# attention_1 of a two-layer decoder: one pass of statistics for two norms, the residual on ScalarE, weights split two heads ahead

## The chip, the core and the metric

The kernel runs on one core of a Trainium2 chip, in one launch. The metric is the device time of that launch in microseconds (us); lower is better. The engines named below are TensorE (PE, matmuls; PEld its weight loads), VectorE (DVE), ScalarE (ACT), GpSimd (POOL) and SyncE (SP, which here only issues DMAs). Each works through its own queue in order and waits on semaphores.

## The reference

Two decoder layers on x of 4 x 256 rows of 256 numbers, six blocks in a row, each added to x. The change touches only the fourth, the attention of the second layer. Cut to it:

```python
def _layernorm(x, axis=-1, eps=1e-05):
    m = jnp.mean(x, axis=axis, keepdims=True)
    v = jnp.var(x, axis=axis, keepdims=True)
    return (x - m) / jnp.sqrt(v + eps)

def _L1_attn_ref(h, wq, bq, wk, bk, wv, bv, wo, bo, ln_g, ln_b):
    residual = h                                    # h is already _layernorm(x)
    mu = jnp.mean(h, axis=-1, keepdims=True)
    var = jnp.mean(jnp.square(h - mu), axis=-1, keepdims=True)
    x = (h - mu) * jax.lax.rsqrt(var + EPS) * ln_g + ln_b
    q, k, v = ...                                   # 16 heads of 128
    q, k = rope(q), rope(k)
    attn = causal softmax(q k / sqrt(128))
    return (attn v) @ wo.T + bo + residual

x = x + _L1_attn_ref(_layernorm(x, axis=-1), ...)
```

So there are an outer norm (of x, giving h) and an inner norm (of h), and x becomes x + h + bo + the sum over 16 heads.

## The kernel before

The 1024 rows lie as 8 tiles of 128 rows (`NT`) in `k.x`; they are handled in two halves of 4 tiles (`HALF`).

**The entry of the block.** VectorE takes the statistics of x (`row_stats`: bn_stats, then bn_aggr into `k.mv`). GpSimd turns variances into reciprocal roots (`inverse_root`, a sum with eps and a power, 128x4 numbers for a half). VectorE makes `hn` = h, takes the statistics of `hn` again, and makes `xn` in two products of three operands for each tile (L177: subtract the mean and multiply by gamma; L182: multiply by the root and add beta). TensorE turns `xn` (`turn_rows`), ScalarE rounds it into the high part `k.xs[0]`, VectorE subtracts into the low part `k.xs[1]`. All large products are three matmuls on such high and low parts (`split_product`, L142).

**Projections.** A "chunk" is one bank of 512 columns: c = 0, 1 are q, c = 2, 3 are k, c = 4 to 7 are v (of two heads at once). There are two banks `pp`, so chunk c+2 waits until chunk c has been read. For q and k, ScalarE writes the halves exchanged (`swap`, two activations, L1723), VectorE multiplies by the cosine and sine tables (`rope`, L1793 on the bank and L1795 on two tiles in SBUF), and GpSimd adds the two (`project`, L1670, the semaphore `chunk`). For head 0 this stands ahead of the loop, and there VectorE also forms x + bo + hn after each rope (`base_tile`, L1783 and L1785, two tiles after each of four chunks).

**The heads.** `step(H)` is one head; the steps 1 to 14 are a hardware loop of seven rounds of two (`heads`), steps 0 and 15 stand outside. Each step has four blocks b, one for each batch entry. In block b TensorE does the scores of (H, b), turns the probabilities of the block before (`turn_P`, L1925), does one or two chunks of head H+1 (`CHUNKS`: q in b = 0, k in b = 1, one chunk of v each in b = 2 and 3), projects out the block two before (`project_out`, three-matmul products on `OT`), and weighs v with the block before (`weigh`). ScalarE copies the turned probabilities, does the exponentials of (H, b) (L1747, L1749), the swaps, and the high part of `OT`. VectorE does the row maxima (L1803, L1805), the low part of `OT` (L135), the ropes, v's bias, and the sum into x (`add_y`, L1834).

**Weights.** SyncE fetches, for each head, `w` (q and k weights and biases, 257 KB) and `wo` (128 KB), and `wv` (256 KB) for each two heads, into one or two buffers. ScalarE rounds each to a high part (`w_to_high`, `wo_to_high`), GpSimd subtracts to the low part (`low`, L1661). In step H the casts of the weights of H+1 are the first thing on ScalarE, and their low parts the first on GpSimd; TensorE's first chunk of the step waits for the low part (`w_split`). On SyncE the order of each round is wv, w (even), wo (even), w (odd), wo (odd); a `wo` waits for `added` of the head before last, so it and everything queued behind it goes out after block 1 of a step.

## Time and profile before

| what | value |
| --- | --- |
| time, three runs | 1245.62, 1249.98, 1250.1 us; median 1249.98 |
| profiled execution | 1249.12 us, its span 1247.3 us |
| TensorE matmul busy | 1052.3 us, 84% of the span |
| VectorE / ScalarE / GpSimd busy | 802.0 / 646.6 / 448.6 us |
| granted TensorE clock, mean | 0.939 of full speed |
| attention_1 in the span | from 662.7 us (first statistics) to 1014.9 us (last sum into x) |

Times in the rows are us from the start of the span; a duration of a merged row covers all its instructions (x4 is four). "idle before" in square brackets is how long the engine had nothing to do just before, and who released it. The attention's tiles show as sb_a_..., since the program's names are shown without numbers.

### The profile page before, as it was taken

To read this page: it belongs to the slowest core of one execution; us is meant where nothing else is said; L and a number is where in the kernel's file an instruction comes from. 1 tells how busy PE (TensorE), PEld (TensorE's weight loads), DVE (VectorE), ACT (ScalarE), POOL (GpSimd) and SP (SyncE) were. 2 spreads that over 40 slices of the span, in tenths; PEclk is the share of its full clock that TensorE was granted. 3 is DMA by queue.
4 is the path that set the end of the run, shared out by engine and by line. 5 is a ranking of instruction groups with operands and counts; after the bars stand their busy time and mean duration, and the time that the engine had idled before them with its cause. 6 is when DMAs were issued, how large, how long until landed. Compare 5 with 4: busy or idle time off the path is not lost. (4 is left out here: it accounts for less than half of the span.)

```text
span 1247.3 us, 21375 instructions
## 1 busy us (share of the span) xinstructions
PE 1052.3 (84%) x7014; PEld 833.8 (67%) x7016; DVE 802.0 (64%) x2260; ACT 646.6 (52%) x1583; POOL 448.6 (36%) x408
## 2 busy tenths in 40 slices
PE   4789999999988986699993799999999977786767
PEld 3556666666665655588882588788887855575556
DVE  5656666666644565355557867677676745489983
ACT  2166676766663751243331566767676642234532
POOL 5456565655634331000002433433343300106730
PEclk8999999999998996799996899999999998898878
DMA  4250212101005000444430001010110000000001
GB/s 135 66 162 18 52 44 51 44 19 35 2 2 193 1 2 0 91 117 111 105 71 13 9 14 34 21 34 17 30 34 21 17 1 0 1 26 26 26 28 45
DMA packets 27246, 53.54 MB, mean 43 GB/s; under 512 B 4565, under 2 KB 11797, under 8 KB 26788
## 3 DMA queue, kind: packets, MB, share of 16 engines
q1 hardware_dynamic: 27172, 52.60, 15.5%
q8 instruction: 41, 0.67, 0.2%
q14 instruction: 33, 0.27, 0.1%
HBM read 42.56 MB, written 1.63 MB: 35 GB/s over the span
## 5 line engine op out<-in xcount | busy, mean ns | idle before, releaser
L382 POOL TENSOR_TENSOR sb_a_P<-sb_a_P,sb_a_rec 128x512 f32<-128x512 f32 x128 | 130.5, 1040 | 134.7 <-DVE sb_a_rec L572 134.7
L459 ACT ACTIVATE sb_a_P<-sb_a_nS,sb_a_nm 128x257 f32<-128x257 f32 x256 | 129.0, 509 | 24.4 <-DVE sb_a_nm L561 24.3
L561 DVE CUSTOM_DVE_ANT_0 sb_a_nS<-a_pS,sb_a_mask,sb_a_nsink 128x256 f32<-128x256 f32 x256 | 107.7, 479 | 15.5 <-PE a_pS L685 15.5
L1723 ACT ACTIVATE sb_a_t<-a_pp,sb_a_w 64x512 f32<-64x512 f32 x128 | 87.5, 684 | 49.4 <-PE a_pp L142 48.1
L468 ACT COPY sb_xn<-a_pT 128x512 f32<-128x512 f32 x128 | 73.7, 576 | 74.7 <-PE a_pT L699 74.5
L142 PE MATMUL a_pp<-sb_x_high,sb_a_w_low 128*128 128x512 f32 x188 | 87.1, 464 | 29.2 <-POOL sb_a_w_low L1661 20.3
L699 PE MATMUL a_pT<-sb_ident,sb_a_P 128*128 128x128 f32 x512 | 82.0, 283 | 18.4 <-ACT sb_xn L468 10.5
L1793 DVE SCALAR_TENSOR_TENSOR sb_a_t<-a_pp,sb_a_w,sb_a_cs 128x512 f32<-128x512 f32 x64 | 47.8, 746 | 73.9 <-ACT sb_a_t L1723 73.9
L699 PEld LDWEIGHTS a_pT<-sb_ident,sb_a_P 128*128 128x128 f32 x512 | 54.4, 142 | 52.1 <-issue 42.0
L142 PE MATMUL a_pY<-sb_a_wo_high,sb_a_OT_low 128*128 128x256 f32 x256 | 79.2, 309 | 7.6 <-DVE sb_a_OT_low L135 5.3
L130 ACT CAST sb_a_OT_high<-a_pO 128x256 fp32r<-128x256 f32 (+1 forms) x96 | 42.6, 444 | 78.1 <-PE a_pO L1936 39.2
L142 PE MATMUL a_pp<-sb_x_low,sb_a_w_high 128*128 128x512 f32 x188 | 76.1, 405 | 0.0
L142 PE MATMUL a_pp<-sb_x_high,sb_a_w_high 128*128 128x512 f32 x188 | 75.8, 403 | 0.0
L1670 POOL TENSOR_TENSOR sb_a_qT<-sb_a_t 128x512 f32<-128x512 f32 x32 | 41.3, 1291 | 91.8 <-DVE sb_a_t L1795 91.8
L142 PE MATMUL a_pY<-sb_a_wo_low,sb_a_OT_high 128*128 128x256 f32 x256 | 71.7, 280 | 0.0
L142 PE MATMUL a_pY<-sb_a_wo_high,sb_a_OT_high 128*128 128x256 f32 x256 | 71.5, 279 | 0.0
L142 PEld LDWEIGHTS a_pp<-sb_x_high,sb_a_w_low 128*128 128x128 f32 x188 | 36.6, 195 | 48.7 <-issue 24.8
L709 PE MATMUL a_pO<-sb_xn,sb_a_v 128*64 128x256 f32 x512 | 68.8, 392 | 0.0
L685 PE MATMUL a_pS<-sb_a_kr,sb_a_qT 32*128 32x256 f32 x1024 | 64.3, 387 | 1.1 <-DMA sb_a_kr<-sb_a_kall 1.1
L195 POOL MEMSET sb_minus_half<- 128x8 f32 x6 | 0.6, 104 | 179.0 <-POOLq L116 178.7
L516 DVE SCALAR_TENSOR_TENSOR sb_xT<-a_pp,sb_a_w,sb_a_cos 128x512 f32<-128x512 f32 x30 | 22.5, 751 | 64.1 <-PE a_pp L142 64.1
L685 PEld LDWEIGHTS a_pS<-sb_a_kr,sb_a_qT 32*128 32x128 f32 x1024 | 49.3, 184 | 15.6 <-issue 11.9
(359 smaller groups left out, 3242.8 us busy)
## 6 DMA issues: line engine op xcount, KB each, us to landing
sb_m_cw<-m_table SPq DMA_DIRECT2D x17, 512.0 KB
sb_a_kr<-sb_a_kall SPq DMA_DIRECT2D x56, 128.0 KB, 2.4
sb_f_w<-f_w SPq DMA_DIRECT2D x12, 384.0 KB, 3.0
sb_m_gu<-m_gu SPq DMA_DIRECT2D x17, 256.0 KB, 6.5
sb_a_w<-a_w SPq DMA_DIRECT2D x16, 257.0 KB, 2.7
sb_m_dn<-m_dn SPq DMA_DIRECT2D x17, 128.0 KB, 6.7
sb_a_w<-a_w SPq DMA_DIRECT2D x8, 259.0 KB, 2.7
sb_a_wo<-a_wo SPq DMA_DIRECT2D x8, 256.0 KB, 2.6
```

Of the source, the lines that this page charges most:

```text
L130: return nc.scalar.copy(out, x)
L142: ins = nc.tensor.matmul(out, a[p], b[q], start=start and i == 0, stop=stop and i == 2, **kw)
L382: nc.gpsimd.tensor_tensor(part, part, rec[b % 2][:, h, :].rearrange("p (q o) -> p q o", o=1) .to_broadcast([P, 2, S]), ALU.mult).then_inc( ...
L459: out = nc.scalar.activation(Pm[b % 2][:, h, qt, 0:S + 1], nS[:, h, qt, 0:S + 1], ACT.Exp, bias=nm[b % 2][:, h, qt:qt + 1], scale=-1.0, ac ...
L468: nc.scalar.copy(PT[h], pT[:, :]).then_inc(PT_ready, 1)
L561: out = nc.vector.tensor_tensor_reduce(nS[:, h, qt, 0:S], pS[h][:, qt * S:(qt + 1) * S], wmask[:, qt, :], -1.0, nsink[par][:, h:h + 1], AL ...
L685: out = nc.tensor.matmul(pS[h][:, qt * S:(qt + 1) * S], qT[par][e][strip, c:c + P], kr[par][e][strip, b * S:(b + 1) * S], start=(e == 0), ...
L699: out = nc.tensor.transpose(pT[:, (2 * c + qt) * P:(2 * c + qt + 1) * P], Pm[b % 2][:, h, qt, c * P:(c + 1) * P], k.tile["ident"][:, :])
L709: out = nc.tensor.matmul(pO[h * A0_D:(h + 1) * A0_D, p * S:(p + 1) * S], values_at(G, 2 * b + c), PT[2 * p + h][:, c * S:(c + 1) * S], sta ...
L1670: nc.gpsimd.tensor_tensor(dst[:, half * NC:(half + 1) * NC], t1[c % 2][:, :, :].rearrange("p b s -> p (b s)"), t2[c % 2][:, :, :].rearrang ...
L1723: out = nc.scalar.activation(t2[n][a, :, :].rearrange("p b s -> p (b s)"), pp[n][b, :], ACT.Identity, bias=bias[b])
L1793: nc.vector.scalar_tensor_tensor(out=t1[n][:, :, :], in0=pp[n][:, :].rearrange("p (b s) -> p b s", b=2), scalar=bias, in1=table(0), op0=AL ...
```

## The change

- The inner norm's statistics are no longer taken from `hn`. From the mean m and variance V of x alone, h = (x - m) r with r = (V + eps)^-1/2, and the inner norm is (x - m) times (V (1 + eps) + eps^2)^-1/2. GpSimd makes both roots in one power on 128x2x4 numbers for each half (`spread2`, `root2`), and VectorE makes `xn` from x in two products a tile. The tile `hn`, its scaling and its statistics are gone.
- x + h is formed as x (1 + r) - m r by one ScalarE activation a tile (`grow`), with `grown` and `shift` made by VectorE; bo is added by GpSimd, eight sums after head 0's last `project` (L1712). VectorE's `base_tile` is gone. VectorE still waits for all eight (`based`) ahead of the first step.
- Weights are split earlier. ScalarE casts `w` of head H+2 in block 2 of step H, `wo` of head H+1 in block 3, and `wv` in block 1 of odd steps. GpSimd makes the low parts of `w` and `wo` after the four projects of H+1, and that of `wv` between the second and the third. The first two heads' `w`, `wv` and `wo` of head 0 are split at the entry. SyncE's order and waits are unchanged.
- The loop now holds steps 1 to 12; the steps 13, 14 and 15 are written out.

```diff
@@ heads
-            with eng.Fori(0, (A1_H - 2) // 2) as i:
+            with eng.Fori(0, (A1_H - 4) // 2) as i:
...
-            step(A1_H - 1, 1, last=True)
+            for H in range(A1_H - 3, A1_H):
+                step(H, H % 2, last=(H == A1_H - 1))
@@ gpsimd
-            for turn in range(2):
-                inverse_root(nc, pool, k, ln, rstd_ready, turn)
+            exponents = k.minus_half[:, :].rearrange("p (a n) -> p a n", a=2)
+            for half in range(2):
+                cols = slice(half * HALF, (half + 1) * HALF)
+                pool.wait_ge(ln, (half + 1) * 2 * HALF)
+                nc.gpsimd.tensor_scalar(spread2[:, 0, cols], k.mv[:, cols, 1], LN_EPS, None, ALU.add)
+                nc.gpsimd.tensor_scalar(spread2[:, 1, cols], k.mv[:, cols, 1], 1.0 + LN_EPS, LN_EPS * LN_EPS,
+                                        ALU.mult, ALU.add).then_inc(rstd_ready, 1)
+                pool.wait_ge(rstd_ready, root_ready(0, half) - 1)
+                nc.gpsimd.tensor_tensor(root2[:, :, cols], spread2[:, :, cols], exponents, ALU.pow).then_inc(rstd_ready, 1)
...
-                if not last:
-                    w_low(H + 1, 1 - par)
-                    if par == 1:
-                        low(wv_high, H + 3, wv[:, :], wvs, wv_split, 2)
-                low(wo_high, H + 1, wo[par][:, 0:D], wos[par], wo_split)
-                if not last:
-                    project(H + 1, 1 - par)
+                project(H + 1, 1 - par, (0, 1))
+                if par == 1:
+                    low(wv_high, H + 3, wv[:, :], wvs, wv_split, 2)
+                project(H + 1, 1 - par, (2, 3))
+                if more(H, 2):
+                    w_low(H + 2, par)
+                wo_low(H + 1, 1 - par)
@@ scalar, entry
+            w_to_high(1, 1)
+            wo_to_high(0, 0)
+                act.wait_ge(shifts, half + 1)
+                for t in range(half * HALF, (half + 1) * HALF):
+                    nc.scalar.activation(k.x[:, t, :], k.x[:, t, :], ACT.Identity, bias=shift[:, t:t + 1],
+                                         scale=grown[:, t:t + 1]).then_inc(grown_x, 1)
@@ vector
-                row_scale(nc, dve, k, k.x, hn, rstd_ready, 0, half, h_ready)
-                dve.wait_ge(h_ready, (half + 1) * HALF)
-                row_stats(nc, dve, k, hn, ln, 1, half)
...
-                nc.vector.tensor_tensor(k.x[:, t, :], k.x[:, t, :], rows[:, 2, :], ALU.add).then_inc(based, 1)
-                dve.wait_ge(based, NT + 2 * t + 1)
-                nc.vector.tensor_tensor(k.x[:, t, :], k.x[:, t, :], hn[:, t, :], ALU.add).then_inc(based, 1)
```

How this moves instructions, at three places. First GpSimd at the entry, ahead of head 0's projections; before:

```order
L202 TENSOR_SCALAR sb_ve<-sb_mv 128x4
L204 TENSOR_TENSOR sb_rstd<-sb_ve,sb_minus_half 128x4
L1661 TENSOR_TENSOR sb_a1_w0_low<-sb_a1_w0,sb_a1_w0_high 128x512
L1661 TENSOR_TENSOR sb_a1_wv_low<-sb_a1_wv0,sb_a1_wv_high 128x512
L1670 TENSOR_TENSOR sb_a1_qT0<-sb_a1_t10,sb_a1_t20 128x512
```

and now:

```order
L1673 TENSOR_TENSOR sb_a1_root2<-sb_a1_spread2,sb_minus_half 128x2x4
L1677 TENSOR_TENSOR sb_a1_w0_low<-sb_a1_w0,sb_a1_w0_high 128x512
L1677 TENSOR_TENSOR sb_a1_wv_low<-sb_a1_wv0,sb_a1_wv_high 128x512
L1677 TENSOR_TENSOR sb_a1_w1_low<-sb_a1_w1,sb_a1_w1_high 128x512
L1677 TENSOR_TENSOR sb_a1_wo0_low<-sb_a1_wo0,sb_a1_wo0_high 128x256
L1689 TENSOR_TENSOR sb_a1_qT0<-sb_a1_t10,sb_a1_t20 128x512
```

Four low parts instead of two now stand between the last power and the first projection's sum.

Second, ScalarE in the loop, from block 3 of one step into block 0 of the next (Pm is the exponential's output, OT the weighed values, PT the turned probabilities); before:

```order
L1749 ACTIVATE sb_a1_Pm1,sb_a1_den3<-sb_a1_nS1,sb_a1_nm1 128x256
L130 CAST sb_a1_OT0_high<-a1_pO0 128x256
L130 CAST sb_a1_w1_high<-sb_a1_w1 128x512
L130 CAST sb_a1_wo0_high<-sb_a1_wo0 128x256
L1741 COPY sb_a1_PT1<-a1_pT 128x384
```

and now the same cast of w stands in block 2 of the step before, ahead of the high part of OT:

```order
L1776 ACTIVATE sb_a1_Pm0,sb_a1_den2<-sb_a1_nS0,sb_a1_nm0 128x256
L1624 ISA
L1723 REGISTER_ALU
L130 CAST sb_a1_w1_high<-sb_a1_w1 128x512
L130 CAST sb_a1_OT1_high<-a1_pO1 128x256
L1768 COPY sb_a1_PT0<-a1_pT 128x384
```

The cast has moved back by some two blocks, and OT's high part stands directly behind it (the two rows without a tile compute what the cast waits for).

Third, GpSimd in an odd step of the loop, now:

```order
L1689 TENSOR_TENSOR sb_a1_qT0<-sb_a1_t11,sb_a1_t21 128x512
L1676 REGISTER_ALU
L1677 TENSOR_TENSOR sb_a1_wv_low<-sb_a1_wv0,sb_a1_wv_high 128x512
L1687 REGISTER_ALU
L1689 TENSOR_TENSOR sb_a1_kT0<-sb_a1_t10,sb_a1_t20 128x512
```

where before wv's low part stood ahead of all four projections:

```order
L1661 TENSOR_TENSOR sb_a1_w0_low<-sb_a1_w0,sb_a1_w0_high 128x512
L1660 REGISTER_ALU
L1661 TENSOR_TENSOR sb_a1_wv_low<-sb_a1_wv0,sb_a1_wv_high 128x512
L1660 REGISTER_ALU
L1661 TENSOR_TENSOR sb_a1_wo1_low<-sb_a1_wo1,sb_a1_wo1_high 128x256
```

It now falls between q's second sum and k's first.

## Rows read from the trace of the kernel before

**Rows 1.** Waits of TensorE from 704 to 1000 us: total, times, longest

```profile
PE a_pp L142 <- POOL sb_a_w_low L1661: 20.3, 14, 1.5
```

**Rows 2.** Timeline, TensorE: turned probabilities and the chunk behind; start, us

```profile
865.34 0.49 PE L1925 MATMUL a_pT<-sb_ident,sb_a_Pm 128*128 128x128 f32 x3
865.59 0.48 PE L142 MATMUL a_pp<-sb_x_high,sb_a_w_low 128*128 128x512 f32 x1
...
878.13 0.49 PE L1925 MATMUL a_pT<-sb_ident,sb_a_Pm 128*128 128x128 f32 x3
880.10 0.50 PE L142 MATMUL a_pp<-sb_x_high,sb_a_w_low 128*128 128x512 f32 x1 [1.47 <-POOL sb_a_w_low L1661]
```

**Rows 3.** Timeline, ScalarE's cast and GpSimd's low part ahead of that chunk

```profile
878.08 0.62 ACT L130 CAST sb_a_w_high<-sb_a_w 128x512 fp32r<-128x512 f32 x1
...
878.77 1.27 POOL L1661 TENSOR_TENSOR sb_a_w_low<-sb_a_w,sb_a_w_high 128x512 fp32r<-128x512 f32 x1 [3.97 <-ACT sb_a_w_high L130]
```

**Rows 4.** Timeline, SyncE: w issued, odd and even step; its landing (L1647)

```profile
852.47 0.33 SPq L1647 DMA_DIRECT2D sb_a_w<-a_w  x1
...
873.21 0.33 SPq L1647 DMA_DIRECT2D sb_a_w<-a_w  x1
...
DMA to landing us min/median/max: 2.6/2.7/3.0
```

**Rows 5.** Timeline, ScalarE in block 2 of those two steps

```profile
853.15 0.19 ACT L1749 ACTIVATION_READ_ACCUMULATOR sb_a_Pm<-sb_a_nS,sb_a_nm 128x1 f32 x1
...
872.68 0.19 ACT L1749 ACTIVATION_READ_ACCUMULATOR sb_a_Pm<-sb_a_nS,sb_a_nm 128x1 f32 x1
873.89 0.37 ACT L130 CAST sb_a_OT_high<-a_pO 128x256 fp32r<-128x256 f32 x1 [1.03 <-PE a_pO L1936]
```

**Rows 6.** Timeline, block 3: VectorE's low part of OT and TensorE's use

```profile
875.35 0.42 DVE L135 TENSOR_TENSOR sb_a_OT_low<-a_pO,sb_a_OT_high 128x256 fp32r<-128x256 f32 x1
...
876.11 0.28 PE L142 MATMUL a_pY<-sb_a_wo_high,sb_a_OT_low 128*128 128x256 f32 x1
```

**Rows 7.** Timeline: the third rope's second half, and v's chunk behind it

```profile
869.76 0.68 DVE L1795 TENSOR_TENSOR sb_a_t<-sb_a_t,sb_a_cs 128x512 f32<-128x512 f32 x1
...
870.71 0.37 PE L142 MATMUL a_pp<-sb_a_wv_high,sb_x_low 128*128 128x256 f32 x1
```

**Rows 8.** Timeline, VectorE at the entry: four products of each kind

```profile
672.44 1.64 DVE L177 SCALAR_TENSOR_TENSOR sb_xn<-sb_a_hn,sb_mv,sb_a_rows 128x256 f32<-128x256 f32 x4
674.00 3.69 DVE L182 SCALAR_TENSOR_TENSOR sb_xn<-sb_xn,sb_rstd,sb_a_rows 128x256 f32<-128x256 f32 x4
```

**Rows 9.** Timeline, GpSimd beside them

```profile
673.06 1.11 POOL L204 TENSOR_TENSOR sb_rstd<-sb_ve,sb_minus_half 128x4 f32<-128x4 f32 x1
674.15 1.45 POOL L1661 TENSOR_TENSOR sb_a_w_low<-sb_a_w,sb_a_w_high 128x512 fp32r<-128x512 f32 x1
675.56 1.44 POOL L1661 TENSOR_TENSOR sb_a_wv_low<-sb_a_wv,sb_a_wv_high 128x512 fp32r<-128x512 f32 x1
```

**Rows 10.** Groups of GpSimd, whole span: busy us, mean ns, idle before

```profile
L412 POOL TENSOR_TENSOR sb_x<-sb_x,sb_a_bo 128x256 f32<-128x256 f32 x8 | 5.6, 733 | 0.0
```

**Rows 11.** Groups from 600 to 1000 us: the swaps and the ropes

```profile
L1723 ACT ACTIVATE sb_a_t<-a_pp,sb_a_w 64x512 f32<-64x512 f32 x128 | 87.5, 684 | 49.4 <-PE a_pp L142 48.1
...
L1793 DVE SCALAR_TENSOR_TENSOR sb_a_t<-a_pp,sb_a_w,sb_a_cs 128x512 f32<-128x512 f32 x64 | 47.8, 746 | 73.9 <-ACT sb_a_t L1723 73.9
L1795 DVE TENSOR_TENSOR sb_a_t<-sb_a_t,sb_a_cs 128x512 f32<-128x512 f32 x64 | 43.6, 681 | 0.0
```

**Rows 12.** Timeline: TensorE's first chunk, VectorE's first row maxima

```profile
682.10 0.80 PE L142 MATMUL a_pp<-sb_x_high,sb_a_w_low 128*128 128x512 f32 x1 [0.42 <-DVE sb_x_low L135]
...
704.27 0.28 DVE L1803 CUSTOM_DVE_ANT_0 sb_a_nS<-a_pS,sb_a_mask 128x128 f32<-128x128 f32 x1
```

**Rows 13.** Timeline, VectorE: a base tile beside GpSimd's sum, and the statistics' end

```profile
665.90 0.38 DVE L156 BATCH_NORM_AGGREGATE sb_mv<-sb_stats 128x2 f32<-128x6 f32 x4
...
688.03 1.40 DVE L1785 TENSOR_TENSOR sb_x<-sb_x,sb_a_hn 128x256 f32<-128x256 f32 x1
```

More of the change, by code:

```diff
@@ L1603, in exists, with more @@
             return not ((first and b < lag) or (drain and b >= lag))
+        def more(H, n):
+            return not isinstance(H, int) or H + n < A1_H
         def before(H, c, n):
@@ L1664, in w_low, with wo_low, project @@
                 low(w_high, X + 1, w[par][:, 0:2 * KD * P], ws[par], w_split)
-            def project(X, par):
-                for c in range(4):
+            def wo_low(X, par):
+                low(wo_high, X + 1, wo[par][:, 0:D], wos[par], wo_split)
+            def project(X, par, cc=range(4)):
+                for c in cc:
                     pool.wait_ge(roped, X * 4 + (c + 1))
@@ L1675, in step @@
             def step(H, par, first=False, last=False, drain=False):
-                if drain:
+                if drain or last:
                     return
-                if not last:
-                    w_low(H + 1, 1 - par)
-                    if par == 1:
-                        low(wv_high, H + 3, wv[:, :], wvs, wv_split, 2)
-                low(wo_high, H + 1, wo[par][:, 0:D], wos[par], wo_split)
-                if not last:
-                    project(H + 1, 1 - par)
+                project(H + 1, 1 - par, (0, 1))
[5 more added lines that the diff above has]
+                wo_low(H + 1, 1 - par)
             w_low(0, 0)
             low(wv_high, 2, wv[:, :], wvs, wv_split, 2)
+            w_low(1, 1)
+            wo_low(0, 0)
             project(0, 0)
+            for t in range(NT):
+                pool.wait_ge(grown_x, t + 1)
+                nc.gpsimd.tensor_tensor(k.x[:, t, :], k.x[:, t, :], rows[:, 2, :], ALU.add).then_inc(based, 1)
             heads(pool, step)
@@ L1709, in _, with grow @@
             high_of(nc, wvs[0][:, :], wv[:, :]).then_inc(wv_high, 2)
-            for j in (0, 2, 1, 3):
-                act.wait_ge(turned, (j % NH2) + 1)
-                high_of(nc, part_of(k.xs[0], j), turn_banks[j][:, :]).then_inc(x_high, 1)
+            w_to_high(1, 1)
+            wo_to_high(0, 0)
+            def grow(half):
+                act.wait_ge(shifts, half + 1)
+                for t in range(half * HALF, (half + 1) * HALF):
+                    nc.scalar.activation(k.x[:, t, :], k.x[:, t, :], ACT.Identity, bias=shift[:, t:t + 1],
+                                         scale=grown[:, t:t + 1]).then_inc(grown_x, 1)
+            for half in range(2):
+                grow(half)
+                act.wait_ge(turned, half + 1)
+                for j in (half, 2 + half):
+                    high_of(nc, part_of(k.xs[0], j), turn_banks[j][:, :]).then_inc(x_high, 1)
             def swap(X, par, c):
@@ L1751, in step @@
                             .then_inc(probs, 1)
+                    if not drain and not last:
+                        if b == 1 and par == 1:
+                            act.wait_ge(wv_in, H * 8 + 8)
+                            act.wait_ge(proj, H * 6 + 6)
+                            high_of(nc, wvs[0][:, :], wv[:, :]).then_inc(wv_high, 2)
+                        if b == 2 and more(H, 2):
+                            w_to_high(H + 2, par)
+                        if b == 3:
+                            wo_to_high(H + 1, 1 - par)
                     if len(cc) > 0 and cc[0] < 4:
```

40 lines of the change are left out of this document (22 added, 18 removed).

## The prediction

> **What bounds the kernel now.** I read the list of waits first, TensorE's alone, over the heads of this attention. One line holds nearly all of it: 14 waits, 20.3 us together, for the low part of the next head's weights [rows 1]. TensorE has no other idle row there, so in this stage TensorE sets the pace and this wait lies on its path. The timeline gives its true price. Without a wait a chunk starts 0.25 us behind the turned probabilities (865.34 to 865.59), with it 1.97 us behind (878.13 to 880.10), so one costs 1.72 us [rows 2]. Its cause is on the page: a cast of 0.62 and a subtraction of 1.27, both begun only at the turn of the step [rows 3]. The second bound is the entry: VectorE is busy almost without a break from 662.8 on, TensorE's first chunk starts at 682.10, and the first row maxima stand at 704.27 [rows 12].
>
> **The change part by part.**
>
> *The wait on the split weights* goes in steps 1 to 14: 14 x 1.72 = 24.1 us [rows 1, 2]. The low parts now start behind the last project of a step, blocks ahead of their use.
>
> *What is late next: the transfer.* SyncE's order is unchanged, so w of head H+2 is still issued only after the sum of block 1 in step H, and now ScalarE wants it in block 2 of the same step. In an even step it is issued at 873.21 and lands 2.7 us later, at 875.9 [rows 4]; ScalarE's exponentials end at 872.87 [rows 5]. Both hang on the same sum of VectorE, so this distance of 3.0 us does not shrink when TensorE gets faster. Behind the waiting cast stands OT's high part. It moves from 873.89 to 875.9 + 0.52 (the cast, until the next can start) = 876.45. Its 0.37 and the low part's 0.42 with two handovers put TensorE's use at 877.3, where it now starts at 876.11 [rows 5, 6]: 1.2 us late. Chunk 5 or 7 of TensorE covers the rest. In an odd step wv is not in between: issue at 852.47, landing 855.2, exponentials over at 853.34 [rows 4, 5], a wait of 1.8; OT's low part is then there at 856.6. TensorE would ask at 856.5 (876.11 less one head; the exponentials lie 19.5 apart [rows 5]), so it is some 0.15 late. Steps 2 to 12, even: 6 x 1.2 = 7.2. Steps 1 to 13, odd: 7 x 0.15 = 1.1. Step 0 has its w long before, step 14 has none to cast. By the row's ends (2.6 and 3.0 us of landing) this sum is 7.4 and 12.
>
> *wv in block 1 of odd steps.* Its cast of some 0.52 stands ahead of the third swap, and its low part of 1.27 to 1.29 on GpSimd lies beside the third rope's second product, which reads two tiles from SBUF. Such a product beside a GpSimd subtraction takes 1.40 instead of 0.42 (one base tile [rows 13]). Here the two overlap only at the end; I reckon 0.15. So the third rope ends 0.67 late. The slack is small: it ends at 870.44 and v's chunk starts at 870.71 [rows 7], so 0.4 reaches TensorE, and VectorE's queue carries the rest to the low part of OT behind it. Bounds: nothing (if the cast falls into idle time) and 0.52 + 0.98; taken 0.65, since slack is shown to be only 0.27. 7 x 0.65 = 4.6.
>
> Loop: 24.1 - 7.2 - 1.1 - 4.6 = 11.2 us gained.
>
> *The entry up to the first chunk.* Statistics end at 666.2 [rows 13]. VectorE then has 16 products at 1.64 for four, 6.5 us in all, and small ones of 0.4, where it now has these plus the scaling and second statistics. Alone they would end at 672.9. But four GpSimd subtractions (some 1.3, 1.3, 1.3 and 0.7 us) now run beside them, from the end of the second power at about 668.4. Rows: beside two of those subtractions four products took 3.69 instead of 1.64 [rows 8, 9], 1.0 for each. Four cost 4.0 at that rate; bounds 2.0 (if only two meet products) and 4.6 (their whole length). The power on 8 numbers a row is not in the trace; 1.11 is that of 4 [rows 9], so it is between 1.1 and 2.2; VectorE works on the first products meanwhile, so it decides only when the subtractions begin. The first two low parts of x follow, 1.2 us: first chunk at 672.9 + 4.0 + 1.2 = 678.1 instead of 682.1 [rows 12]. Gain 4.0.
>
> A rule speaks of the same resource. By the row, GpSimd's power of 1.11 at 673.06 did not stretch the four products of 1.64 beside it, while its subtractions did [rows 8, 9]. The Trainium skill, "SBUF — State Buffer", section "Who interferes with whom", has VectorE with two SBUF inputs and any GpSimd instruction that reads SBUF exclude each other for the whole instruction. Were that so for the powers too, products would stand still for one or both of them and this gain would be 1 to 2.5 us smaller; the row decides against it.
>
> *From the first chunk to the first maxima:* 22.2 us now [rows 12]. The base tiles leave VectorE, up to 1.40 + 0.42 each [rows 13]. What is left is a ring: chunk about 1.5 (2.7 for the first, whose matmul shows 0.80 against 0.50 us [rows 2, 12]), swap 2 x 0.68, rope 0.75 + 0.68 [rows 11], then TensorE's next chunk into the same bank. Up to the first rope's end 2.8 + 1.4 + 1.4 = 5.6; one turn of the ring (4.4) later the third, at 10.0; the fourth 2.0 behind; GpSimd's last sum 1.3 more: 13.3. But now eight sums of bo stand behind it, 8 x 0.733 = 5.9 [rows 10], and VectorE waits for all of them before its first maxima: 19.2. Gain 3.0. In step 0 ScalarE no longer trails base tiles, which I count as 0.5. If VectorE did not have to wait, 5 more would be gained; the wait is in the program, so they are not.
>
> *ScalarE's eight activations on x* (some 0.4 each) lie in its idle time before the turned tiles arrive, and the two extra casts at the entry too: nothing, or at most 0.5 if the second half's four hold up the rounding. The small VectorE operations are in the 0.4. Steps 13 and 14 written out instead of looped: nothing, no stall shows in step 15 now.
>
> **Sum:** 11.2 + 4.0 + 3.5 = 18.7 us. The profiled execution took 1249.1 us (span 1247.3), so it would take 1230.4; the median of the runs lies 0.9 above it, which gives 1231.
>
> **The rivals.**
>
> *The weights come in time, or GpSimd hinders less.* If the cast did not wait, 8.3 fewer are lost; if wv's parts are hidden, 4.6; if the subtractions at the entry cost half, 2. With the first and half of the rest it is about 1249.98 - 18.7 - 11.5 = 1220. For it: TensorE's slack in these blocks is only estimated. Against: issue and exponentials hang on one VectorE sum, 0.3 us apart, against 2.7 of landing.
>
> *The casts' wait passes whole to TensorE.* ScalarE's lateness, less the 1.03 it idles there today [rows 5], is 2.5 in even steps and 1.3 in odd ones: 6 x 2.5 + 7 x 1.3 = 24.1, as much as was removed. Less the 4.6 it leaves 2.9 to 7.5 us of the entry: 1242 to 1247, middle 1245. It needs the exponentials of block 3, behind the same cast, to be what TensorE waits for; they are used a block later, which speaks against it.
>
> *Slower: the transfer misses its turn and feeds itself.* The landing rows hold for bursts that ScalarE does not wait on. If ScalarE's lateness delays VectorE's sums, these delay SyncE's `wo`, w goes out later, and the cast waits again. Each us past the slack costs TensorE nearly one in 13 steps. Zero gain is reached at a landing of 2.7 + 18.7 / 13 = 4.1 us; at 4.8 it is 1258. The rows end at 3.0 [rows 4], and the sum of block 1 does not stand behind the cast of block 2, so the ring is broken within a step.
>
> *It does not do what it says:* the wait stays because w's low part is late for another reason. By the rows it is ready at 875.9 + 0.65 + 1.27 = 877.8 in an even step, and the first chunk of the next would stand at 878.4 + 1.2 = 879.6 [rows 2 to 4]: 1.7 us in hand, so a landing of 4.4 us would bring it back.
>
> **How the numbers follow.** The forecast (1226 to 1238) 0.62; in time or less hindrance, 1220, 0.18; whole wait passed on, 1245, 0.12; slower, 1258, 0.05; the wait stays, about 1243 to 1250, 0.03. The range takes the first two and the faster edge of the third: 1219 to 1243. About 0.5% is what a measurement here can tell from no change, so under 1243.7 is faster: 0.62 + 0.18 + 0.04 of the third = 0.84. Within 0.5%: 0.08 + 0.03 = 0.11. Slower: 0.05.
>
> **What would show it.** Right: no wait of the first chunk for the low weights; in block 2 ScalarE's cast of w with 3.0 us idle in even steps and 1.8 in odd, released by the DMA; TensorE idle about 1.2 us before the second projection out of even steps, and 0.3 to 0.4 before v's first chunk of odd ones; first chunk at 678; eight sums of 0.73 on GpSimd with VectorE idle before its first maxima; a head 0.8 us shorter on average (11.2 / 14). Wrong: a cast without idle time, products at the entry near 0.4 us each, or a landing above 3.0 us. Then the time goes to 1220, or to 1245 and above.

## The result, and the profile after the change

The changed kernel takes 1232.47 us (median of four runs, 1230.88 to 1235.94) against 1250.04 us for the kernel before: a ratio of 0.9871, 95% interval 0.9841 to 0.9902. The forecast was 1231 us with a range of 1219 to 1243. The total came out as forecast, but the sum behind it did not: the loop gave 6.4 us instead of 11.2. Why the total was met all the same comes first, since it decides how everything else is read.

**The total holds a part that the change did not make.** The change touches nothing ahead of this attention's norms. Yet these norms, whose first instruction is VectorE's first statistics (line 153), began at 662.76 us in the profile of before and at 659.08 in that of after. A second trace of each kernel (both under the experiments) began at 664.01 and 663.85, and over all 14 profiles of this study the start lies between 658.87 and 664.01, in no order by kernel. So I measure the stage by itself: from its first statistics to the first statistics of the stage behind it. Here are the two rows for before, then for after. Timelines give start, length, engine, line, operation, and in brackets the idle time before and what ended it.

```profile
662.76 1.40 DVE L153 BATCH_NORM_STATS2 sb_stats<-sb_x 128x6 f32<-128x256 f32 x4 [1.99 <-PEq L116]
...
1015.46 1.41 DVE L153 BATCH_NORM_STATS2 sb_stats<-sb_x 128x6 f32<-128x256 f32 x4 [0.53 <-PEq L1536]
```

```profile
659.08 1.41 DVE L153 BATCH_NORM_STATS2 sb_stats<-sb_x 128x6 f32<-128x256 f32 x4 [1.99 <-PEq L116]
...
999.00 1.41 DVE L153 BATCH_NORM_STATS2 sb_stats<-sb_x 128x6 f32<-128x256 f32 x4 [0.53 <-PEq L1536]
```

The stage took 352.70 us and takes 339.92: **12.8 us gained, where the sum said 18.7.** The other 3.7 us between the two profiles were there before the changed code ran. The stages behind it take 231.8 us in both (span less the second row).

Inside the stage I mark each step by its first row maxima (their start in block 0 of head H; [rows 12] have the first of them). "Step H" below is the time from head H's mark to head H+1's. All in us, from the timelines:

| | first chunk after start | first maxima after start | step 0 | steps 1, 3 .. 13 (sum of 7) | steps 2, 4 .. 12 (sum of 6) | step 14 | stage |
|---|---|---|---|---|---|---|---|
| before | 19.34 | 41.51 | 17.45 | 137.47 | 117.53 | 19.56 | 352.70 |
| after | 14.94 | 34.22 | 18.35 | 133.54 | 116.56 | 18.04 | 339.92 |
| gained | 4.40 | 7.29 | -0.90 | 3.93 | 0.97 | 1.52 | 12.78 |

Three views of after say where the rest of the 24 us went. First the waits of TensorE and of ScalarE between 704 and 990 us (total, times, longest), to be held against [rows 1]:

```profile
PE a_pY L142 <- DVE sb_a_OT_low L135: 10.2, 10, 1.5
PE a_pp L142 <- DVE sb_a_t L1833: 3.0, 7, 0.5
...
ACT sb_a_w_high L130 <- DMA sb_a_w<-a_w: 32.9, 13, 3.5
```

The wait for w's low part is gone, all 14 of it. Two others stand in its place on TensorE (of the 10.2 us, 7.2 are six waits in even steps and 0.16 one in step 1; the other three, 0.94 each, belong to the last head, which shows them in the kernel before as well), and ScalarE now waits 32.9 us for the transfer of w. Then the timeline, the parts that answer to [rows 4] to [rows 7]: an even step from w's issue to the projection out, and an odd one.

```profile
859.38 0.33 SPq L1656 DMA_DIRECT2D sb_a_w<-a_w  x1
862.17 0.62 ACT L130 CAST sb_a_w_high<-sb_a_w 128x512 fp32r<-128x512 f32 x1 [3.13 <-DMA sb_a_w<-a_w]
862.69 0.37 ACT L130 CAST sb_a_OT_high<-a_pO 128x256 fp32r<-128x256 f32 x1
863.57 0.39 PE L142 MATMUL a_pY<-sb_a_wo_high,sb_a_OT_low 128*128 128x256 f32 x1 [1.12 <-DVE sb_a_OT_low L135]
...
875.80 1.03 DVE L1833 TENSOR_TENSOR sb_a_t<-sb_a_t,sb_a_cs 128x512 f32<-128x512 f32 x1
876.96 0.38 PE L142 MATMUL a_pp<-sb_a_wv_high,sb_x_low 128*128 128x256 f32 x1 [0.47 <-DVE sb_a_t L1833]
881.40 0.62 ACT L130 CAST sb_a_w_high<-sb_a_w 128x512 fp32r<-128x512 f32 x1 [2.07 <-DMA sb_a_w<-a_w]
```

Even step: ScalarE idles 3.13 us in front of the cast of w, OT's high part stands behind that cast, and TensorE waits 1.12. Odd step: the rope's second product takes 1.03 us, where it took 0.68 [rows 7], and v's chunk starts 0.47 late; ScalarE's wait for w is 2.07.

Last the entry, which answers to [rows 8, 9, 12]: VectorE's products, GpSimd beside them, and what follows.

```profile
665.81 4.70 DVE L1819 SCALAR_TENSOR_TENSOR sb_xn<-sb_xn,sb_a_root,sb_a_rows 128x256 f32<-128x256 f32 x4
670.43 0.69 DVE L1815 TENSOR_SCALAR sb_a_grown<-sb_a_root 128x4 f32<-128x4 f32 x1
674.02 0.80 PE L142 MATMUL a_pp<-sb_x_high,sb_a_w_low 128*128 128x512 f32 x1 [0.42 <-DVE sb_x_low L135]
...
693.30 0.29 DVE L1841 CUSTOM_DVE_ANT_0 sb_a_nS<-a_pS,sb_a_mask 128x128 f32<-128x128 f32 x1 [4.63 <-POOL sb_x L1712]
695.01 0.90 PE L1961 MATMUL a_pT<-sb_ident,sb_a_Pm 128*128 128x128 f32 x3 [2.96 <-ACT sb_a_Pm L1776]
697.80 0.80 PE L142 MATMUL a_pp<-sb_x_high,sb_a_w_low 128*128 128x512 f32 x1 [1.89 <-DVE sb_a_t L1833]
```

VectorE idles 4.63 us for GpSimd's eight sums before its first maxima. TensorE then waits 2.96 and 1.89, and its matmul of 128x512 takes 0.80 us (0.50 at [rows 2]). Step 0 became longer by these waits and by the granted clock behind them: it was half (the lower level, 1.2 GHz) in the two us from 697 on, columns as in the windows view (length, busy of PE, PEld, DVE, ACT, POOL, then the clock, the DMA's share and GB/s):

```profile
697.00:699.00 2.00, 1.20 (x3) 1.01 (x4) 2.00 (x8) 1.90 (x6) 1.17 (x1) 0.50 0.00 0
```

### The profile page after: what moved, and what is told of

The parts are those of the page before. It is cut to its first block and busy times, and to the rows that moved or that the text cites. A ratio compares the mean times of both kernels' runs of the same rounds, so it can differ in the third digit from the quotient of the medians.

```text
span 1230.8 us, 21280 instructions
## 1 busy us (share of the span) xinstructions
PE 1050.8 (85%) x7014; PEld 829.6 (67%) x7016; DVE 791.5 (64%) x2224; ACT 649.0 (53%) x1591; POOL 453.7 (37%) x414
## 5 line engine op out<-in xcount | busy, mean ns | idle before, releaser
L142 PEld LDWEIGHTS a_pY<-sb_a_wo_high,sb_a_OT_low 128*128 128x128 f32 x256 | 48.2, 188 | 25.0 <-DVE sb_a_OT_low L135 22.7
L135 DVE TENSOR_TENSOR sb_a_OT_low<-a_pO,sb_a_OT_high 128x256 fp32r<-128x256 f32 (+1 forms) x96 | 49.0, 511 | 23.7 <-ACT sb_a_OT_high L130 20.1
```

The source lines that it names most:

```text
L135: return nc.vector.tensor_tensor(out, x, high, ALU.subtract)
L142: ins = nc.tensor.matmul(out, a[p], b[q], start=start and i == 0, stop=stop and i == 2, **kw)
```

## The experiments

Twelve kernels were run: ten variants, and the kernel before and the changed one once more. Each is read by the stage's length and its steps, which do not contain what differs from run to run ahead of the stage; the ratio to the kernel before stands beside it (none where a kernel was timed in one execution only). From the first statistics, in us:

| kernel | first chunk | first maxima | step 0 | odd (7) | even (6) | step 14 | stage | ratio, 95% |
|---|---|---|---|---|---|---|---|---|
| before, second trace | 19.35 | 41.69 | 17.27 | 137.29 | 117.47 | 19.51 | 352.37 | |
| changed, second trace | 14.94 | 34.24 | 18.38 | 133.93 | 116.30 | 18.05 | 340.13 | 0.9885 (0.9867 to 0.9903) |
| w first | 14.94 | 34.20 | 18.42 | 131.63 | 107.72 | 18.04 | 329.25 | 0.9828 (0.9804 to 0.9851) |
| wv at the top | 14.93 | 34.21 | 18.48 | 127.91 | 116.01 | 18.03 | 333.88 | 0.9841 (0.9806 to 0.9875) |
| wait put off | 14.93 | 29.68 | 17.20 | 133.89 | 116.14 | 18.04 | 334.18 | 0.9855 (0.9827 to 0.9884) |
| these three | 14.93 | 29.32 | 17.24 | 125.70 | 107.71 | 18.04 | 317.25 | 0.9707 (0.9682 to 0.9733) |
| w first, cast of wv at the top | 14.94 | 34.20 | 18.38 | 131.55 | 107.73 | 18.05 | 329.14 | |
| w later | 14.93 | 34.23 | 18.49 | 149.31 | 137.66 | 18.05 | 376.97 | 1.0221 (1.0194 to 1.0249) |
| low parts later at the entry | 13.40 | 34.15 | 18.53 | 134.00 | 116.20 | 18.03 | 340.15 | |
| norms only | 13.40 | 32.19 | 20.02 | 138.27 | 117.69 | 19.56 | 346.94 | 0.9925 (0.9900 to 0.9949) |
| weights only | 20.83 | 42.47 | 16.73 | 133.93 | 116.32 | 17.86 | 346.47 | 0.9928 (0.9902 to 0.9955) |
| all four edits | 13.40 | 27.67 | 19.08 | 125.72 | 107.75 | 18.05 | 317.52 | 0.9717 (0.9692 to 0.9741) |

**How far the stage's length can be trusted.** Both kernels once more.

> The kernel before, once more, for a second trace of it. Theory (the 3.7 us by which the attention stage began earlier in the changed kernel's profile come from executions that differ, since no instruction ahead of it was changed): its first statistics start anywhere from 659 to 663.5 us, and the stage takes 352.7 us within 0.3. Rival (the stage itself scatters that much): a stage length more than 1 us away from 352.7.

> The changed kernel, once more, for a second trace and more rounds on this chip. Theory: first statistics anywhere from 659 to 663.5 us, the stage 339.9 us within 0.7 (its odd and even steps hang on transfers that scatter by some 0.1 us each), a ratio of 0.985 to 0.990 to the kernel before. Rival (the stage scatters as the total does): a stage more than 1.5 us away from 339.9.

The stage repeats within 0.33 us (352.70 and 352.37, a hair outside the 0.3 I had named) and 0.21 us (339.92 and 340.13). The starts were 664.01 and 663.85, 0.4 to 0.5 us outside the range that I had given, and the ratio is 0.9885. So the change is worth 12.2 to 12.8 us, about 1.0%, which lies inside both intervals of the ratio (12.5 / 1249 is a ratio of 0.990). The 3.7 us belong to those two executions and not to the change. Earlier marks, the first statistics of the stages ahead, say where they arise: at 378.34 and 377.65 the two profiles were 0.7 us apart, at 478.97 and 475.34 already 3.6. The windows view of the same ten us of that stage, before and then after, shows what differs, TensorE's granted clock:

```profile
398.34:408.34 10.00, 10.00 (x58) 6.51 (x58) 4.64 (x10) 6.57 (x9) 3.31 (x3) 0.69 0.00 0
```

```profile
397.65:407.65 10.00, 10.00 (x92) 6.73 (x93) 6.81 (x16) 8.25 (x12) 4.13 (x3) 1.00 0.00 0
```

A clock of 0.69 for ten us takes 3.1 us of work away, about the 2.9 by which the stage is longer. Over the 14 profiles three have the low clock at this place (before, changed second trace, wait put off) and take 100.6 to 100.8 us there; the other eleven have 1.00 and take 97.7 to 98.9. Why the clock falls there in some executions of equal code stays open.

**Is it the transfer?** w leaves a head earlier. SyncE's transfers stand in three functions here, with the waits that they had; w of head 2 is issued ahead of the loop, and the last round is written out.

```diff
+            fetch_w(2, 0)
             with sp.Fori(0, (A1_H - 4) // 2) as i:
                 fetch_wv(i)
                 for s in range(2):
-                    fetch_w(i * 2 + (2 + s), s)
+                    fetch_w(i * 2 + (3 + s), 1 - s)
                     fetch_wo(i * 2 + (2 + s), s)
```

> The changed kernel, but SyncE issues w of head H+3 before it waits with wo of head H+2, so w leaves a whole head earlier; nothing else is moved and nothing is left out. Theory (the late transfer is what the loop lost): ScalarE's 32.9 us of idle time before its 13 casts of w go to nearly nothing; the 6 even steps, which lost 1.39 us each against a step without a new wait, get it back (8.3 us), and the odd ones a small part (0 to 2 us): the attention stage takes 330 to 332 us instead of 339.9, the whole kernel 8 to 10 us less than the changed one, a ratio of about 0.979 to the kernel before. Rival (the casts themselves hurt where they stand now, ahead of the exponentials of block 3, and the wait for the DMA only covers that): the idle time goes too, but the stage gets less than 3 us shorter, 337 us or more.

The six even steps fell from 116.56 to 107.72 (8.8 us, 17.95 each), the seven odd ones from 133.54 to 131.63 (1.9). The stage is 10.7 us shorter, a little more than the 8 to 10 expected, and ScalarE has no wait for a DMA left between 704 and 985 us. TensorE's waits, in the list from 720 to 960 us, are down to the odd steps' one:

```profile
PE a_pp L142 <- DVE sb_a_t L1849: 3.0, 7, 0.5
```

The theory holds: the late transfer cost 8.8 us in even steps and 1.9 in odd ones. The casts themselves, where they stand, cost nothing once their data is there.

**And if w comes later still?** 128 KB into a spare buffer, waited for, ahead of each w.

```diff
+                    sp.dma_start(spare[:, :], src["a1_wo"][0]).then_inc(spare_in, 16)
+                    sp.wait_ge(spare_in, (h - 1) * 16)
                     sp.dma_start(w[s][:, :], src["a1_w"][bass.ds(h, 1)].rearrange("g p n -> p (g n)"))\
```

> The changed kernel, but ahead of every w SyncE first brings 128 KB into a spare buffer and waits until they are there, which took 2.0 us for wo in the trace of the changed kernel: w lands about 2.1 us later in each of the 13 steps that fetch one. Nothing is left out. Theory (no slack is left, and the delay is paid once per step, one for one, as the prediction's slower rival has it from a landing of 4.1 us on): 13 x 2.1 = 27 us on the stage, 365 to 369 us instead of 339.9, the kernel slower than the one before, about 1258 us. The cast of w then waits some 2 us longer, and in even steps the first chunk's wait for w's low part comes back. Rival (the wait feeds itself: each late w makes the next one later still): more than 35 us, with waits for the DMA that grow from step to step. Rival (ScalarE's lateness is mostly covered): less than 14 us.

The kernel is slower than the one before, 1274.63 us, ratio 1.0221; the stage takes 376.97 us, 37.1 more than the changed one. Expected were 27, so this missed, and by size it fits the rival that feeds itself. By its own sign it does not: the even steps take 23.38, 23.10, 23.01, 22.81, 22.85 and 22.51 us and the odd ones 21.05 to 21.67, with no growth. The rows tell the two parts apart: issue, cast, use of OT in an even step, and the first matmul behind it.

```profile
880.87 0.33 SPq L1659 DMA_DIRECT2D sb_a_w<-a_w  x1
883.51 0.62 ACT L130 CAST sb_a_w_high<-sb_a_w 128x512 fp32r<-128x512 f32 x1 [5.38 <-DMA sb_a_w<-a_w]
884.91 0.39 PE L142 MATMUL a_pY<-sb_a_wo_high,sb_a_OT_low 128*128 128x256 f32 x1 [3.38 <-DVE sb_a_OT_low L135]
885.72 0.97 PE L1973 MATMUL a_pO<-sb_a_PT,sb_a_v 128*128 128x256 f32 x2
...
886.00:888.00 2.00, 2.00 (x8) 1.76 (x7) 0.80 (x2) 0.37 (x1) 0.73 (x1) 0.50 0.00 0
```

ScalarE's wait rose from 3.13 to 5.38 in this even step; over all of them it rose by 2.25 on average in the even steps (32.7 us in six against 19.2) and by 2.06 in the odd ones (28.1 in seven against 13.6). One for one that makes 6 x 2.25 + 7 x 2.06 = 27.9 us, about the amount expected. The odd steps paid 2.25 each (15.8 / 7), 0.2 above their delay, the even ones 3.52 (21.1 / 6), 1.3 above theirs. The larger excess has TensorE's clock in it: behind the idle time of 3.38 us the clock granted is 0.50 from 886 to 888 and 0.70 from 888 to 890, which takes 1.0 + 0.6 = 1.6 us of work away. The wait of the odd step ahead of it is 2.00 us (at 863.30), and its clock stays at 1.00:

```profile
863.30:865.30 2.00, 2.00 (x14) 1.92 (x15) 1.49 (x4) 1.37 (x6) 1.30 (x2) 1.00 0.00 0
```

All thirteen are alike: behind the six waits of the even steps (3.37 to 3.62 us) the clock fell to 0.50, behind the seven of the odd steps (1.95 to 2.22 us) it never left 1.00. So the slower rival of the prediction had the price of a us nearly right (2.25 paid for 2.06 where the clock held), but not the feeding back on itself that it was named for, and it lacked the second price behind a long wait. Its last worry, w's low part late again, did not come true: TensorE has no wait for it here.

**What do wv's two parts cost?** Both back at the top of odd steps.

```diff
+                if not drain and not last and par == 1:
+                    act.wait_ge(wv_in, H * 8 + 8)
+                    act.wait_ge(proj, H * 6 + 6)
+                    high_of(nc, wvs[0][:, :], wv[:, :]).then_inc(wv_high, 2)
...
-                project(H + 1, 1 - par, (0, 1))
                 if par == 1:
                     low(wv_high, H + 3, wv[:, :], wvs, wv_split, 2)
+                project(H + 1, 1 - par, (0, 1))
```

> The changed kernel, but in odd steps the cast of wv and its low part stand at the top of the step again, where the kernel before has them, ahead of all projects; nothing is left out. Theory (wv in block 1 costs 0.65 us an odd step, as the prediction has it, and more by the steps after: 1.04 us each in all): the stage gets 4 to 5 us shorter (335 to 336 us), all of it in the 7 odd steps. Rival (the odd steps lose their 1.04 us to w's cast, which waits 2.0 us for its transfer there too): less than 1.5 us.

The odd steps fell by 5.6 us (133.54 to 127.91, 0.80 each), the stage by 6.0. That is more than the 4 to 5 expected and far from the rival's 1.5. With w first the same thing reads more clearly: odd steps 131.63, against 125.70 with both edits, are 0.85 each. To see which of the two parts it is, w first with only ScalarE's cast at the top:

```diff
+                if not drain and not last and par == 1:
+                    act.wait_ge(wv_in, H * 8 + 8)
+                    act.wait_ge(proj, H * 6 + 6)
+                    high_of(nc, wvs[0][:, :], wv[:, :]).then_inc(wv_high, 2)
```

> The changed kernel with w issued a head earlier, and of wv's two parts only ScalarE's cast back at the top of odd steps; GpSimd's low part stays between the second and the third projection. Nothing is left out. Odd steps took 18.82 us with both parts in block 1 and 17.96 with neither. Theory (ScalarE's cast, 0.61 us ahead of the third swap, is the larger part, as the prediction has it with 0.52 against 0.15): odd steps 18.1 to 18.3 us. Rival (GpSimd's low part, which holds up the rope's second product by 0.35 and the third projection behind it, is the larger part): 18.4 us or more.

The odd steps did not move: 131.55 against 131.63. My theory fell and the rival holds: with the low part where it is, moving the cast gives nothing back, and the 0.85 us go only when the low part moves too. (The cast alone in block 1, with the low part out of the way, was not run, so what it would cost by itself stays open.) The rows show how. GpSimd's subtraction and VectorE's second product of the third rope, first with the cast in block 1 (w first), then with the cast at the top:

```profile
868.57 1.03 DVE L1849 TENSOR_TENSOR sb_a_t<-sb_a_t,sb_a_cs 128x512 f32<-128x512 f32 x1
...
867.76 1.29 POOL L1693 TENSOR_TENSOR sb_a_wv_low<-sb_a_wv,sb_a_wv_high 128x512 fp32r<-128x512 f32 x1
```

```profile
871.04 1.54 DVE L1849 TENSOR_TENSOR sb_a_t<-sb_a_t,sb_a_cs 128x512 f32<-128x512 f32 x1
...
870.75 1.28 POOL L1693 TENSOR_TENSOR sb_a_wv_low<-sb_a_wv,sb_a_wv_high 128x512 fp32r<-128x512 f32 x1
```

The subtraction ends at 869.05 and at 872.03, the product at 869.60 and at 872.58, so in both 0.55 us behind the subtraction. Without the cast in its way the product starts half a us sooner within the step and is held half a us longer. A product with two inputs in SBUF makes next to no headway while GpSimd subtracts, and does most of its 0.68 afterwards. It is so in all seven odd steps of both kernels: the product ends 0.54 to 0.56 us behind the subtraction. The Trainium skill, "SBUF — State Buffer", section "Who interferes with whom", says the same: of a VectorE instruction with two SBUF inputs and a GpSimd instruction that reads SBUF, the one issued second waits until the other is through. In these traces, where GpSimd's subtraction is the one issued first, it holds.

**What does the early wait for bo's sums cost?**

```diff
+                if isinstance(H, int) and H == 0:
+                    dve.wait_ge(based, NT)
                 if not before(H, u, A1_U):
                     dve.wait_ge(added, H * A1_U + u)
...
-            dve.wait_ge(based, NT)
             heads(dve, step)
```

> The changed kernel, but VectorE's wait for the eight sums of bo stands directly ahead of its first addition to x (head 0, block 0) instead of ahead of its first row maxima; nothing is left out. Theory (the wait itself holds up step 0, since VectorE idles 4.63 us there): the first maxima come 3.5 to 4.5 us earlier, TensorE's idle time behind them in step 0 (2.96 and 1.89 us) and its half clock go with it, and the stage gets 3.5 to 5 us shorter. Rival (the wait only moves: VectorE then waits in block 0 of head 0, because GpSimd does these sums ahead of the next head's projections, which TensorE and ScalarE need anyway): less than 1.5 us shorter.

The first maxima come 4.5 us sooner (29.68 instead of 34.22 behind the start), and step 0 takes 17.20 instead of 18.35. The stage is 5.7 us shorter, above the 3.5 to 5 expected. Nothing waits for these sums later, and the matmul that took 0.80 us takes 0.50 at full clock:

```profile
692.22 0.29 DVE L1841 CUSTOM_DVE_ANT_0 sb_a_nS<-a_pS,sb_a_mask 128x128 f32<-128x128 f32 x1
...
697.14 0.50 PE L142 MATMUL a_pp<-sb_x_high,sb_a_w_low 128*128 128x512 f32 x1 [1.33 <-DVE sb_a_t L1833]
```

The prediction had the 5 us in hand ("the wait is in the program, so they are not" gained) but not that the same wait also lengthens step 0. How the 1.15 us of step 0 divide between the waits and the clock is not shown.

**Do GpSimd's subtractions hold up the entry?** Two of the four go behind the projections of head 0.

```diff
-            w_low(1, 1)
-            wo_low(0, 0)
             project(0, 0)
+            w_low(1, 1)
+            wo_low(0, 0)
```

> The changed kernel, but GpSimd makes the low parts of w of head 1 and of wo of head 0 behind the projections of head 0 instead of ahead of them; nothing is left out. Theory (each GpSimd subtraction beside VectorE's products at the entry holds them up by about 1 us; there were four, now two meet them): the four products that took 4.70 us take 3.6 to 3.9, the small scaling behind them 0.16 instead of 0.69, and TensorE's first chunk starts 13.2 to 13.6 us behind the first statistics instead of 14.94. The first row maxima do not move by more than 1 us, since they wait for the eight sums of bo, which now stand 2.3 us of other work later in GpSimd's queue: the stage stays within 1 us of 339.9. Rival (the products are long for another reason, such as ScalarE's activations on the same x): they stay at 4.7 us and the first chunk at 14.9.

```profile
666.52 3.69 DVE L1819 SCALAR_TENSOR_TENSOR sb_xn<-sb_xn,sb_a_root,sb_a_rows 128x256 f32<-128x256 f32 x4
670.13 0.15 DVE L1815 TENSOR_SCALAR sb_a_grown<-sb_a_root 128x4 f32<-128x4 f32 x1
673.19 0.79 PE L142 MATMUL a_pp<-sb_x_high,sb_a_w_low 128*128 128x512 f32 x1 [0.42 <-DVE sb_x_low L135]
...
693.94 0.29 DVE L1841 CUSTOM_DVE_ANT_0 sb_a_nS<-a_pS,sb_a_mask 128x128 f32<-128x128 f32 x1 [6.52 <-POOL sb_x L1712]
```

All as the theory said: 3.69 us instead of 4.70, 0.15 instead of 0.69, the first chunk 13.40 behind the start, and nothing won, since VectorE now idles 6.52 for the sums (stage 340.15).

**The two halves of the change.**

> Only the norms' part of the change: one pass of statistics, x formed by ScalarE and GpSimd; the weights are split as in the kernel before, at the top of a step. Nothing is left out. Theory (the two parts are separate, and the entry is worth what its rows say): from the first statistics to the first maxima 33 to 34.5 us instead of 41.5, steps 1 to 14 as before (19.6 each, 274.6), the stage 343 to 347 us instead of 352.7. Rival (the gain at the entry rests on the split two heads ahead, since otherwise w's low part stands behind eight sums of bo in step 0): step 0 takes 20 us or more instead of 17.45, and the stage 348 us or more.

> Only the weights' part of the change, on the kernel before: heads' weights split two steps ahead in blocks 1 to 3, norms and residual as in the kernel before. Nothing is left out. Theory (the loop is worth 6.4 us by the rows: 14 waits of 1.65 gone, late transfers and wv take 16 back): steps 1 to 14 together 268 us, as in the changed kernel; the entry up to 1.5 us longer, by two more GpSimd subtractions beside VectorE; the stage 345.5 to 348 us. Rival (the losses in the loop belong to the changed entry, for instance a shifted beat between VectorE and SyncE): steps 1 to 14 near 17.96 each, 252 us, and the stage under 333 us.

Norms alone gain 5.8 us (352.70 to 346.94), weights alone 6.2 (to 346.47); together 12.0, and the change gains 12.8. Steps 1 to 14 of norms alone take 275.5 us, 1.0 more than before, which nothing here explains. Weights alone have the loop of the changed kernel (133.93 + 116.32 + 17.86 = 268.1 in steps 1 to 14, as the theory had it), so its losses do not come from the new entry. At the entry it loses 1.5 us up to the first chunk, the same four products taking 4.70 us there too. Norms alone reach the first maxima at 32.19, earlier than the 33 to 34.5 expected, but half of the rival is true: step 0 takes 20.02, because w's low part for head 1 stands behind the eight sums and TensorE waits for it.

```profile
696.71 0.77 PE L142 MATMUL a_pp<-sb_x_high,sb_a_w_low 128*128 128x512 f32 x1 [5.78 <-POOL sb_a_w_low L1676]
...
689.84 5.50 POOL L1709 TENSOR_TENSOR sb_x<-sb_x,sb_a_rows 128x256 f32<-128x256 f32 x8
```

So the split of head 1 at the entry costs the norms 1.5 us up to the first chunk and 2.0 up to the first maxima (34.22 against 32.19), and spares them 1.7 in step 0 (18.35 against 20.02). Up to head 1's first maxima that is 52.57 against 52.21: at this place it is no gain.

**The three edits together.** w first, wv's parts at the top, the wait put off.

> The changed kernel with all three edits: w issued a head earlier, wv's parts back at the top of odd steps, VectorE's wait for bo's sums put off to its first addition; nothing is left out. Theory (three separate losses that add): the sum of the three, 15 to 19 us off the stage (321 to 325 us instead of 339.9), 1213 to 1217 us for the kernel, ratio 0.972 to 0.975 to the kernel before. Rival (they share one cover, and with one of them gone VectorE or ScalarE sets the pace of a head): at most 11 us, and every step 1 to 13 ends at one length of about 18.5 us or more.

The stage takes 317.25 us, 22.7 less than the changed kernel; the three alone gave 10.7 + 6.0 + 5.7 = 22.4. They add in full, which is more than I had dared to expect, and the kernel takes 1211.86 us, ratio 0.9707 (0.9682 to 0.9733). Three marks of it, and the windows view of the loop (busy of PE first):

```profile
816.34 0.29 DVE L1857 CUSTOM_DVE_ANT_0 sb_a_nS<-a_pS,sb_a_mask 128x128 f32<-128x128 f32 x1 [0.64 <-PE a_pS L1970]
834.31 0.29 DVE L1857 CUSTOM_DVE_ANT_0 sb_a_nS<-a_pS,sb_a_mask 128x128 f32<-128x128 f32 x1 [0.66 <-PE a_pS L1970]
852.27 0.29 DVE L1857 CUSTOM_DVE_ANT_0 sb_a_nS<-a_pS,sb_a_mask 128x128 f32<-128x128 f32 x1 [0.66 <-PE a_pS L1970]
...
720.00:960.00 240.00, 240.00 (x1558) 215.62 (x1556) 181.40 (x562) 181.50 (x460) 102.37 (x86) 1.00 0.10 28
```

Steps 1 to 13 take 17.91 to 17.97 us each and TensorE is busy for all of the 240 us. This is the loop with TensorE never idle, the measure for what each wait really cost.

**And the fourth edit on top** (the two low parts behind the projections of head 0):

> All three edits (w issued a head earlier, wv's parts at the top of odd steps, VectorE's wait put off) and the fourth, the two low parts behind the projections of head 0; nothing is left out. Theory (with VectorE's early wait gone, an earlier first chunk reaches the first maxima): first maxima about 1.5 us earlier than without the fourth, stage 315.5 to 316.5 us against 317.25, kernel 1209 to 1212 us. Rival (the low parts for head 1, now later, make step 0 longer by as much): no difference, 317 us or more.

The first maxima come 1.65 us earlier (27.67 against 29.32) and step 0 takes 1.84 longer: 317.52 us, no gain. The rival holds. Its step 0 shows where: the chunk of head 1 waits for w's low part, later ones for the ropes.

```profile
691.09 0.47 PE L142 MATMUL a_pp<-sb_x_high,sb_a_w_low 128*128 128x512 f32 x1 [0.37 <-POOL sb_a_w_low L1693]
695.70 0.49 PE L142 MATMUL a_pp<-sb_x_high,sb_a_w_low 128*128 128x512 f32 x1 [0.59 <-DVE sb_a_t L1849]
702.22 0.39 PE L142 MATMUL a_pp<-sb_a_wv_high,sb_x_low 128*128 128x256 f32 x1 [1.82 <-DVE sb_a_t L1849]
```

## Why the prediction was right, and where its steps were not

| term of the sum | predicted | measured | from |
|---|---|---|---|
| 14 waits for w's low part | 24.1 | 23.11 | steps 1 to 14, before (274.56) less the three edits (251.45) |
| transfer of w, even steps | -7.2 | -8.84 | after less w first |
| transfer of w, odd steps | -1.1 | -1.91 | after less w first |
| wv in block 1 | -4.6 | -5.94 | w first (257.39) less the three edits (251.45) |
| entry to first chunk | 4.0 | 4.40 | after |
| first chunk to first maxima | 3.0 | 2.89 | after |
| step 0 | 0.5 | -0.90 | after |
| sum | 18.7 | 12.81 | stage |

**The waits** went as said. Their price was a little high: 1.65 us each, by steps of 19.6 against 17.96, where two gaps in the trace had given 1.72. ("TensorE has no other idle row there" is too strong: the same view of 704 to 1000 us has two more rows, 2.2 and 0.9 us, one wait each. Both lie outside steps 1 to 14, and the sum does not use them.)

**The transfer** was the right mechanism, and its signs in the trace were as forecast: ScalarE idle 3.13 us in even steps (3.0 forecast) and 2.07 in odd ones (1.8), TensorE 1.12 us late before the projection out (1.2). What failed is the last step of the working, that TensorE's lateness at OT is the price. The waits shown were 1.03 to 1.47 us in the even steps, 7.2 together, just what the sum has (6 x 1.2), but an even step cost 1.47 on average (8.8 / 6). In odd steps "some 0.15 late" was really 0.27 (1.9 / 7), and only the first of the seven shows a wait for it, 0.16. (A slip beside it: at a landing of 2.6 us the working gives 7.0, not 7.4.) The row of a wait gives less than the wait costs. In this loop it is so for each kind: 1.45 shown and 1.65 paid for w's low part, 0.43 shown and 0.85 paid for v's chunk (3.0 / 7). What makes up the rest was not traced.

**wv** was sized at 0.65 an odd step and cost 0.85, and the working behind it was wrong in both halves. The cast, taken at 0.52 on the path, cost nothing measurable beside the low part; GpSimd's low part, taken at 0.15 because "the two overlap only at the end", was the one that held the product. I had let the product and the subtraction share, a factor on the overlap. In fact one stands still for the other, and the end of the product hangs on the end of the subtraction. (The row that the working rests on, 1.40 us in [rows 13], stands beside one of GpSimd's sums, not a subtraction; the effect is the same.)

**The entry** was right in its mechanism and nearly in size: four products 3.06 us late and a small scaling 0.53 late, together 3.6 against 4.0. Read one by one, three of the four products took 1.48 or 1.49 us instead of 0.48, one beside each of the first three subtractions, and the fourth subtraction met the small scaling; this is the second of the three:

```profile
667.62 1.48 DVE L1819 SCALAR_TENSOR_TENSOR sb_xn<-sb_xn,sb_a_root,sb_a_rows 128x256 f32<-128x256 f32 x1
```

So the rate of 1.0 for each was right, and the fourth cost half of it. The first chunk came 14.94 us behind the start of the stage; the prediction's 678.1 is 15.3 on the same scale (its own parts, 666.2 + 6.5 + 0.4, give 673.1 where it has 672.9).

**Step 0** had the wrong sign. The prediction counted the wait of VectorE before its first maxima as a gain not made. It missed that TensorE, which reaches the first scores while VectorE still waits, idles 2.96 us and 1.89 us, and runs at half clock around and behind these waits. With the wait put off step 0 takes 1.15 us less.

**The total.** That the forecast of 1231 lay within 1.5 us of the median was luck, two errors that offset each other: 5.9 us too much in the sum, and a difference of 3.7 us ahead of the stage between the two profiled executions, most of it from TensorE's clock in a stage that the change does not touch (the rest is the medians' own scatter). The second set of runs gave 1235.64 against 1249.15. By the stages a fair value is 1249.98 - 12.5 = 1237.5, inside the range of 1219 to 1243 and faster by 1.0%. Of the rivals, "in time or less hindrance" is refuted, "the whole wait passed on" too (its 2.9 to 7.5 us of gain against 12.8), and the slower one came true as soon as w landed 2 us later, though not by feeding itself. The last, that the wait stays, is refuted as well: none of the 14 is left, and none came back with w 2 us later, where the prediction had expected it from 1.7 us on.

## What to carry to other kernels

When work is moved ahead, move its data too: the split went a head earlier, its transfer did not, and of 23 us freed 11 went back for that; issuing w a head earlier costs nothing and returned all of it. Give a waiting instruction its place by its first real consumer (here the first addition to x, not the loop's entry), and put a GpSimd subtraction or sum where VectorE has no product with two SBUF inputs on the path beside it. Judge a change of one stage by marks inside that stage when the rest of the program scatters by as much as the effect.
